# Context attention of a decoder: max units and shifts in one stream over all blocks, 128-row tiles in the first maxima, values made in the first norm's block

## What is computed

```python
x = _layernorm(x + _L0_attn_ref(x, ...))          # a Mamba block
x = _layernorm(x + _L0_xattn_ref(x, ctx, ctx, w_q, w_kv, w_concat))
x = _layernorm(x + _L0_ffn_ref(x, ...))           # experts
x = _layernorm(x + _L1_attn_ref(x, ...))          # self attention
x = _layernorm(x + _L1_xattn_ref(ctx, ctx, x, ...))
x = _layernorm(x + _L1_ffn_ref(x, ...))           # experts
```

```python
c = jnp.concatenate([mem, kv], axis=1)            # both are the context
qh = (q @ w_q).reshape(B, L, 16, 8).transpose(0, 2, 1, 3)
k, v = (c @ w_kv)[..., :8], (c @ w_kv)[..., 8:]
attn_prob = softmax(einsum('bhid,bjd->bhij', qh, k) / sqrt(8), axis=-1)
out = einsum('bhij,bjd->bhid', attn_prob, v)
return out.transpose(0, 2, 1, 3).reshape(B, L, 128) @ w_concat
```

## Time and profile before

| | |
|---|---|
| median of 3 runs | 2247.23 us (2247.16 to 2249.95) |
| the profiled execution | 2255.29 us, its span 2253.6 us |
| PE matmul busy | 2100.2 us, 93% |
| DVE busy | 1590.2 us, 71% |
| ACT busy | 1319.3 us, 59% |
| POOL busy | 120.0 us, 5% |
| mean granted TensorE clock | 0.952 |

### The profile page before, as it was taken

One profiled execution on the slowest core, in us unless ns is written; L12 is line 12 of the kernel. 1 busy time (PEld: TensorE's weight loads), 2 busy tenths in 40 slices (PEclk: granted clock), 3 DMA queues, 4 the chain that ended last, 5 costly groups with the idle time before them and its releaser, 6 DMA issues. The chain is left out here.

```text
span 2253.6 us, 38636 instructions
## 1 busy us (share of the span) xinstructions
PE 2100.2 (93%) x15240; PEld 995.6 (44%) x15240; DVE 1590.2 (71%) x2158; ACT 1319.3 (59%) x2189; POOL 120.0 (5%) x156
## 2 busy tenths in 40 slices
PE   8777999999999999999999999899589997999898
PEld 5223343333333333333333333477533333777755
DVE  4997578898888988889888882223778873444335
ACT  4232157777777777777777778533247773333421
POOL 1560000000000000000000000000200010000000
PEclk7898599999999999999999999899779999999989
DMA  4110000000000000000000000011000000000011
GB/s 135 56 65 0 0 1 1 1 1 1 1 1 1 1 1 1 1 1 1 1 1 1 1 1 1 13 33 35 1 1 1 0 0 0 1 1 0 1 33 33
DMA packets 22978, 24.59 MB, mean 11 GB/s; under 512 B 5728, under 2 KB 20224, under 8 KB 22576
## 3 DMA queue, kind: packets, MB, share of 16 engines
q1 hardware_dynamic: 21648, 20.44, 3.0%
q10 hardware_dynamic: 1184, 2.10, 0.2%
HBM read 21.81 MB, written 0.59 MB: 10 GB/s over the span
## 5 line engine op out<-in xcount | busy, mean ns | idle before, releaser
L959 DVE TENSOR_REDUCE sb_max_partial<-ps_max_ps 128x1 f32<-128x1024 f32 (+1 forms) x896 | 958.1, 1107 | 110.1 <-PE ps_max_ps L802 104.4
L950 ACT ACTIVATE sb_probs<-ps_score_ps 128x512 f32<-128x512 f32 (+1 forms) x1632 | 885.3, 595 | 237.9 <-PE ps_score_ps L922 195.2
L802 PE MATMUL ps_max_ps<-sb_key_stack,sb_q_stack 64*128 64x512 f32 (+1 forms) x1664 | 608.5, 443 | 21.7 <-DVE sb_max_partial L959 9.1
L922 PE MATMUL ps_score_ps<-sb_q_stack,sb_key_stack 64*128 64x512 f32 x1632 | 592.5, 442 | 1.9 <-issue 0.4
L903 PE MATMUL ps_acc_ps<-sb_probs,sb_val_ones 128*32 128x256 f32 x6528 | 521.4, 391 | 0.9 <-ACT sb_probs L950 0.4
L922 PEld LDWEIGHTS ps_score_ps<-sb_q_stack,sb_key_stack 64*128 64x128 f32 x1632 | 241.0, 185 | 281.1 <-ACT sb_probs L950 266.3
L802 PEld LDWEIGHTS ps_max_ps<-sb_key_stack,sb_q_stack 64*128 64x128 f32 x1664 | 256.9, 188 | 159.1 <-DVE sb_max_partial L959 135.3
L903 PEld LDWEIGHTS ps_acc_ps<-sb_probs,sb_val_ones 128*32 128x32 f32 x6528 | 128.4, 108 | 293.0 <-ACT sb_probs L950 218.6
L1654 DVE TENSOR_REDUCE sb_s_max_partial<-ps_s_max_ps 128x1 f32<-128x512 f32 x256 | 170.2, 690 | 42.5 <-PE ps_s_max_ps L1579 35.7
L1644 ACT ACTIVATE sb_s_probs<-ps_s_score_ps 128x1024 f32<-128x1024 f32 x128 | 131.0, 1024 | 49.0 <-PE ps_s_score_ps L1616 46.6
L1871 DVE TENSOR_SCALAR_CACHE_REDUCE sb_x_scores<-ps_x_score_ps 128x1024 f32<-128x1024 f32 (+1 forms) x56 | 62.1, 1111 | 80.7 <-PE ps_x_score_ps L1812 80.7
(11 more groups left out here) (279 smaller groups left out, 1738.7 us busy)
## 6 DMA issues: line engine op xcount, KB each, us to landing
sb_val<-c_rows SPq DMA_DIRECT2D x16, 512.0 KB, 3.7
sb_e_w<-L_ffn_rW SPq DMA_DIRECT2D x30, 128.0 KB, 2.0
sb_e_w<-L_ffn_W_T SPq DMA_DIRECT2D x24, 128.0 KB, 2.1
sb_ctx_T<-ctx_T SPq DMA_DIRECT2D x1, 1664.0 KB, 7.8
sb_ctx_T<-ctx_T ACTq DMA_DIRECT2D x1, 1538.0 KB, 8.7
sb_x_T<-x_T SPq DMA_DIRECT2D x1, 512.0 KB, 4.0
sb_x_tok<-x ACTq DMA_DIRECT2D x1, 512.0 KB, 11.0
sb_e_w<-L_ffn_sW SPq DMA_DIRECT2D x4, 128.0 KB, 3.7
```

What stands on the lines that cost most here:

```text
L802: ins = nc.tensor.matmul(max_ps[:, u % 2, a:a + n], q_stack[rows(blk), blk // 2, h * P:(h + 1) * P], k.key_stack[rows(blk), c0 + a:c0 + a ...
L922: nc.tensor.matmul(score_ps[:, e % 3, :], k.key_stack[rows(blk), c * P:(c + 1) * P], q_stack[rows(blk), blk // 2, j * HALF:(j + 1) * HALF] ...
L950: nc.scalar.activation(probs[0:n, c % 3, j * HALF:(j + 1) * HALF], score_ps[0:n, e % 3, :], ACT.Exp).then_inc(exp_done, 1)
L959: nc.vector.tensor_reduce(partial[:, h, r:r + 1], max_ps[:, u % 2, 0:RANGES[r][1]], AX.X, ALU.max).then_inc(unit_used, 1)
```

## The change

- **Values**: all 51 value tiles are made on PE in norm0's block, ahead of the turns of the normed tiles; ACT copies them behind the two copies of `x_T`. Mamba no longer makes them or waits for them.
- **Queries**: the high part is now subtracted by PE (a matmul with `minus_low`, a diagonal of -1 and 0, that adds to the same bank), and ACT copies the bank a second time. DVE has no part in it. The order of makes, subtractions and units is given by two tables; jobs start with the eleventh unit.
- **First maxima**: POOL copies block 0's queries of each head into `q_first`, whose lower 64 rows are zero, and block 0's units are matmuls of 128 rows.
- **One stream**: units and shifts of all blocks stand in one list `order`, where the shift of block b follows the second unit of block b+1. `chunk_of` spreads the items from block 1 on over all chunks: the shift of block b comes in chunk 46 of block b-1. Places in `max_ps` go by position in the list, the shift takes one of them, and an item waits until the one two before it was used; for a shift that is `q_ready`. In a chunk the first item stands between scores and `weigh`, the others behind `weigh`.
- **Shift copy**: ACT, not DVE, copies the turned shift into `q_stack`, after the exponentials of the chunk behind the one with the shift. `partial` and `part2` have two buffers.

```diff
+            nc.vector.tensor_scalar(k.minus_low[:], k.ident[:], k.half_sel_q[:], None, ALU.mult)
...
-def residual_norm(k, tag, branch, added=False, store=None, turned=None):
+def residual_norm(k, tag, branch, added=False, store=None, turned=None, on_pe=None, on_act=None):
...
+                if on_act is not None:
+                    on_act(act)
...
+                if on_pe is not None:
+                    on_pe(pe)
...
-                keys.values(pe, w_kv, range(0, 12))
...
-                keys.values(pe, w_kv, range(12, NCH))
...
-                pe.wait_ge(keys.v_taken, 1)
...
-                keys.take_values(dve)
...
-        residual_norm(k, "norm0", out_ps, turned=wide(4))
+        residual_norm(k, "norm0", out_ps, turned=wide(4), on_pe=lambda pe: keys.values(pe, w_kv), on_act=keys.take_values)
...
+            FEW = 2
+            LAG = 1
+            order = [(0, u) for u in range(UNITS)] + [(0, None)]
+            for b in range(1, NB):
+                order += [(b, u) for u in range(UNITS)]
+                if b > 1:
+                    order.insert(len(order) - UNITS + FEW, (b - 1, None))
+            order.append((NB - 1, None))
+            place = {x: i for i, x in enumerate(order)}
...
+            FIRST = place[(0, None)] + 1
+            SHIFT_AT = 46
+            lead = place[(1, None)] - FIRST + 1
+            chunk_of = {}
+            for i, x in enumerate(order[FIRST:]):
+                if i < lead:
+                    chunk_of[x] = i * SHIFT_AT // (lead - 1)
+                else:
+                    chunk_of[x] = SHIFT_AT + (i - lead + 1) * NCH // (UNITS + 1)
+            items_at = [[x for x in order[FIRST:] if chunk_of[x] == g] for g in range(NB * NCH)]
...
+            def free_place(pe, item):
+
+                if place[item] < 2:
+                    return
+                blk, u = order[place[item] - 2]
+                if u is None:
+                    pe.wait_ge(q_ready, blk + 1)
+                else:
+                    pe.wait_ge(unit_used, blk * UNITS + u + 1)
...
+                    if blk == 0:
+                        ins = nc.tensor.matmul(dst, q_first[:, h * P:(h + 1) * P], k.key_stack[:, c0 + a:c0 + a + n],
+                                               start=True, stop=True)
...
             def turn_shift(pe, blk):
 
+                free_place(pe, (blk, None))
                 pe.wait_ge(parts_ready, blk + 1)
                 for h in range(HB):
-                    ins = nc.tensor.transpose(shift_ps[0:2, h * P:(h + 1) * P], part2[:, h, :].bitcast(F32), k.ident[:])
+                    ins = nc.tensor.transpose(max_ps[0:2, place[(blk, None)] % 2, h * P:(h + 1) * P],
+                                              part2[:, blk % 2, h, :].bitcast(F32), k.ident[:])
                 ins.then_inc(shift_turned, 1)
...
+            def subtract_high(pe, i):
+
+                pe.wait_ge(q_high, i + 1)
+                nc.tensor.matmul(q_bank(i), k.minus_low[:], q_rows(i), start=False, stop=True,
+                                 skip_group_check=True).then_inc(q_minus, 1)
...
-            FIRST_JOB = 8
+            FIRST_JOB = 10
...
+            EARLY = 3
+            MADE_AT = {0: 3, 2: 4, 4: 5, 6: 6, 8: 7, **{11 + 5 * i: HB + i for i in range(HB)}}
+            MINUS_AT = {0: 2, 1: 3, 3: 4, 5: 5, 7: 6, 9: 7, **{12 + 5 * i: HB + i for i in range(HB)}}
...
-                    if with_max and c <= LAST:
-                        max_unit(pe, blk + 1, u)
-                        u += 1
-                    if c >= 1:
-                        weigh(pe, blk, c - 1)
+                    for item in items[:1]:
+                        issue(pe, item)
+                    if c >= LAG:
+                        weigh(pe, blk, c - LAG)
                     elif blk > 0:
-                        weigh(pe, blk - 1, NCH - 1)
-                    if with_max and c in after_weighing:
-                        max_unit(pe, blk + 1, u)
-                        u += 1
-                    if with_max and c == NCH - 2:
-                        turn_shift(pe, blk + 1)
+                        weigh(pe, blk - 1, NCH - LAG + c)
+                    for item in items[1:]:
+                        issue(pe, item)
...
+            def take_shift(act, blk):
+
+                act.wait_ge(shift_turned, blk + 1)
+                lo = HALF_P * (blk % 2) + TERMS
+                nc.scalar.copy(q_stack[lo:lo + 2, blk // 2, :], max_ps[0:2, place[(blk, None)] % 2, :]).then_inc(q_ready, 1)
...
+                    if blk < NB - 1 and blk * NCH + c == chunk_of[(blk + 1, None)] + 1:
+                        take_shift(act, blk + 1)
...
                 @block.tensor
                 def _(pe):
...
+                    make_queries(pe, 0)
+                    for i in range(EARLY - 1):
+                        make_queries(pe, i + 1)
+                        subtract_high(pe, i)
...
                         if u % NR == 0:
-                            pe.wait_ge(q_done, u // NR + 1)
+                            pe.wait_ge(first_ready, u // NR + 1)
...
+                @block.gpsimd
+                def _(pool):
+                    nc.gpsimd.memset(q_first[HALF_P:P, :].bitcast(F32), 0.0)
+                    for h in range(HB):
+                        pool.wait_ge(q_done, h + 1)
+                        nc.gpsimd.tensor_copy(q_first[0:HALF_P, h * P:(h + 1) * P],
+                                              q_stack[0:HALF_P, 0, h * P:(h + 1) * P].bitcast(F32)).then_inc(first_ready, 1)
```

More of the change, by code:

```diff
@@ L350, in make, with values @@
         nc.tensor.matmul(self.bank(r), k.wk_rep[:], k.ctx_T[:, c0:c0 + n], start=True, stop=True).then_inc(self.k_made, 1)
-    def values(self, pe, w_kv, chunks):
+    def values(self, pe, w_kv):
         nc, k = self.k.nc, self.k
-        for c in chunks:
+        for c in range(NCH):
             n = P if c < NCH - 1 else TAIL
-            if c in (0, self.CUT):
-                pe.wait_ge(self.ctx_loaded[1 if c else 0], 16)
             ins = nc.tensor.matmul(self.v_ps[0:n, c, :], k.ctx_T[:, c * P:c * P + n], w_kv[:, HD:2 * HD], start=True,
                                    stop=True)
-        if NCH - 1 in chunks:
-            ins.then_inc(self.v_ready, 1)
+        ins.then_inc(self.v_ready, 1)
     def high_on_act(self, act, r):
@@ L807, in max_unit @@
-            def max_unit(pe, blk, u):
-                for a in (0, HALF):
-                    max_half(pe, blk, u, a)
+                free_place(pe, (blk, u))
+                for a in range(0, cols, HALF):
+                    n = min(HALF, cols - a)
+                    dst = max_ps[:, place[(blk, u)] % 2, a:a + n]
+                    if blk == 0:
+                        ins = nc.tensor.matmul(dst, q_first[:, h * P:(h + 1) * P], k.key_stack[:, c0 + a:c0 + a + n],
+                                               start=True, stop=True)
+                    else:
+                        ins = nc.tensor.matmul(dst, q_stack[rows(blk), blk // 2, h * P:(h + 1) * P],
+                                               k.key_stack[rows(blk), c0 + a:c0 + a + n], start=True, stop=True)
@@ L816, in turn_shift, with issue @@
                 ins.then_inc(shift_turned, 1)
+            def issue(pe, item):
+                if item[1] is None:
+                    turn_shift(pe, item[0])
+                else:
+                    max_unit(pe, *item)
             def q_bank(i):
-                return (score_ps[0:SPAN2, i % 4, :] if i % 4 < 3 else acc_ps[0:SPAN2, :]) if i < HB else score_ps[0:SPAN2, i % 2, :]
+                if i < HB:
+                    return score_ps[:, i % 4, :] if i % 4 < 3 else acc_ps[:]
+                return score_ps[:, i % 2, :]
@@ L997, in _ @@
                     for blk in range(NB):
-                        attend(pe, blk, blk < NB - 1)
-                    weigh(pe, NB - 1, NCH - 1)
+                        attend(pe, blk)
+                    for v in range(NCH - LAG, NCH):
+                        weigh(pe, NB - 1, v)
                 @block.scalar
```

110 lines of the change are left out of this document (46 added, 64 removed).

## The result

The changed kernel took 2332.06 us (median; 2328.43 to 2334.62) beside 2248.59 for the old one on the same chip: ratio 1.0362, 95% interval 1.0331 to 1.0392, slower by 83.5 us. The forecast was 2351, in a range of 2240 to 2450. The profiled execution has a span of 2328.6, 75.0 above that of the old profile (2253.6).

The account below looks back on a forecast made before the run. PE was taken to bound the attention. Values -3.1, first maxima -34.9, stream +44 and clock +98 sum to +104 us on the median 2247.23: 2351, range 2240 to 2450 (the forecast's own 2295 to 2400).

Parts of the forecast that it names:

- Values beside norm0: Value matmuls moved from Mamba to norm0: Mamba ends 15.0 us earlier, norm0 pays 11.9, together -3.1 (-8.7 to +1.9).
- First maxima: First query to first score, at full clock: 78.4 us against 113.3, -34.9 (-38 to -28; 0 if the clock stays low).
- The stream: Units and shifts spread over all attention blocks: 161 us against 117, +44 (+38 to +50), before the clock's cost.
- (a): Attention chunks with two units: 12 x 0.83 us in block 0, 5 x 0.83 = 4.15 in each other.
- (b): Chunks 44 to 50: six units on the scores' own 64 rows no longer hidden, 0.46 us each, 2.8 a block.
- (c): Chunk 47: second unit behind the shift waits for ACT's copy; PE idles 2.0 us, chunk takes 3.88, +2.65.
- (d): Clock falls at each of 14 stalls at chunk 47, rising some 2.4 ordinary chunks later: 7.0 us a stall, 98 in all.
- Rival C: No stall at chunk 47, as ACT's shift copy is done before PE asks: 2222 us (2205 to 2235); chance 0.12.
- B: Rival: the clock holds through the stalls at chunk 47: 2253 us (2240 to 2266); chance 0.14.
- D: Rival: clock falls and does not rise inside a block: +150 to +585 for the 98, 2400 to 2840; chance 0.14.

Follow-up runs that it names:

- experiment 7: Values back in Mamba, in a kernel with the changed start and old attention blocks: 2218.58 us; values alone moved in the old kernel: 2236.34 us, ratio 0.9956.
- experiment 6: Changed kernel with 64-row tiles in the first maxima: 2342.75 us; then changed start with old attention blocks, but the queries' subtraction back on DVE: 2226.93 us.
- experiment 1: Changed kernel with ACT's copy of the shift taken one chunk earlier, behind the exponentials of chunk 46: 2222.67 us, ratio 0.9895.
- experiment 2: Early units (chunks 44 to 50) on the other 64 rows: changed kernel with ACT's shift copy one chunk earlier, 2196.37 us; changed kernel with stall kept, 2259.68 us.
- experiment 5: Changed kernel's first part (values, queries, first maxima) with the old kernel's attention blocks: 2218.07 us, ratio 0.9867.
- experiment 4: Changed kernel with ACT's shift copy one chunk earlier, plus two extra ACT copies behind chunk 25's exponentials: 2252.07 us, ratio 1.0032.
- experiments 2 and 3: The latter of the two: changed kernel with the weighing of chunk 46 issued ahead of the waiting unit at chunk 47; 2318.84 us, ratio 1.0303.

## Why the prediction was right, and where it was off

**Values beside norm0** (-15.0 + 11.9 = -3.1). Norm0's first statistics come at 171.62 instead of 186.85 (-15.2), the first query at 191.05 instead of 193.47 (-2.4). The 102 records took 17.63 for the forecast 16.5, about 4.3 us of it at full clock (forecast 5):
```profile
170.17 17.63 PE L363 MATMUL ps_mamba_ps<-sb_w_kv,sb_ctx_T 128*128 128x8 f32 x102 [0.33 <-PEq L499]
187.73 1.97 PE L202 MATMUL ps_mamba_ps<-sb_ident,sb_x_tok 128*128 128x128 f32 x8
```
Busy time and clock over the same records:
```profile
170.20:174.50 4.30, 4.30 (x39) 4.30 (x40) 3.89 (x20) 1.42 (x2) 0.00 (x0) 1.00 0.00 0
174.50:187.80 13.30, 13.30 (x66) 13.24 (x66) 2.27 (x9) 0.00 (x0) 0.00 (x0) 0.50 0.01 2
```
(The late group of value matmuls in the old trace has 78 records, where the prediction counts 76; no term uses it.) Right in its parts; as a gain on the whole kernel it shows only in the old first maxima (experiment 7).

**First maxima** (78.4 from first query to first score). Measured 270.36 - 191.05 = 79.3: 5.5 to the first unit (forecast 7.4), 67.9 to the end of the last reduce (65), of which 13.0 are the first ten units (13) and 54.9 the other 46 (52), 5.9 behind it (6.0). The size was right, the reason for the full clock half right. I had it that full-height tiles take away the half-empty work that kept the clock low; experiment 6 shows 64-row tiles at full clock too, once the subtraction is on PE. The height of the tiles alone is worth 8.5 us, not the clock's share of 34.9. The rule weighed there, that a change of tiling mode drains the engine (the Trainium skill, TensorEngine Tiling, Key Properties), asked for a fall from 59 to 49 over the last 46 units. In the runs they took 61.0 with 64-row tiles (experiment 6) and 54.9 with 128-row tiles: the direction agrees, 6 of the 10 us are there, and that a drain is what costs them isn't shown.

**The stream.** (a) and (b): without stall and fall the attention is 5.7 longer than before (experiment 1), where the terms gave 44 - 14 x 2.2 = 13. That comes from (b) in the main: forecast 2.8 a block, measured 2.1 (experiment 2). I had priced all six chunks at 0.46; three of them cost that, chunk 46 cost 0.57, and chunks 48 and 50 only 0.24 and 0.12, while at chunk 47 the same rows gave 0.22 back. (c): chunk 47 takes 3.88, as forecast, in the six blocks where the clock is still full through it, and 4.81 in the other eight, the 0.9 more that (d) had for it; 3.88 against experiment 1's 1.59 is 2.3 for the stall, forecast 2.2. Rival C, which is experiment 1 in all but name, had been priced at 2222 and measured 2222.67. That close a hit is luck: C took 38 off for the first part and put 13 on for the stream, where the runs have 30 by the ratio (experiment 5) and 5.7.

**(d) The clock** was the term mis-sized. It fell at each of 14 stalls, as forecast. The attention grew by 1234.4 - 1129.6 = 104.7 from experiment 1, 7.5 a stall; less 2.3 for the stall itself, 5.2 are left for the clock, 73 in all instead of 98. Chunks 48 and 49 at low clock took 3.01, as priced. Three things were too dear: the clock rose in the second chunk of the next block (the first took 2.17, the second 1.38 to 2.08) and not after 2.4 chunks; in six of the blocks it fell only during chunk 48; and chunk 50, with its 260-column unit, took 2.37 and not 3.0. The other eight look like block 3, where the unit behind the stall already runs at half clock and S(48) comes 4.8 after S(47):
```profile
574.70 0.62 PE L954 MATMUL ps_score_ps<-sb_q_stack,sb_key_stack 64*128 64x512 f32 x2
577.34 1.22 PE L836 MATMUL ps_max_ps<-sb_key_stack,sb_q_stack 64*128 64x512 f32 x2 [2.02 <-ACT sb_q_stack L974]
...
579.50 1.22 PE L954 MATMUL ps_score_ps<-sb_q_stack,sb_key_stack 64*128 64x512 f32 x2
```
The 2.4 chunks were a choice between a quick rise (42 us in all) and none (45 for each stall); no row of the old trace gave them, so that the sum came this near is in part luck.

So -25 of the 32 us by which the attention's growth missed the forecast is this term, and -7.5 is (b) with (a).

**The rivals.** B fell: the clock fell at 41 of 42 stalls of 1.5 to 2.3 us (and at the 14 of experiment 6's first kernel, 2.0 each). The Trainium skill (TensorE: Matmul & The Clock Gate, the table on why this matters) warns only of longer idle gaps; here the measurement decides, and it speaks against reading that as leave for shorter ones. Only experiment 4's 1.1 us pauses behave by it. D fell: the clock was back early in each next block. That S and M then fill both halves of the array fits experiment 2, where the same from chunk 48 on cut the low stretch to 3.4 or 6.8 us, but wasn't tested by itself. D's price left a factor out: 45 chunks at 0.925 more in 13 blocks are 541 us at most, not 585.

**The sum.** In the profiles +75.0 against +104; on the medians +83.5, as the old kernel's profiled execution was 6.7 above its median of 2248.59 and the changed kernel's 1.3 below its own. The terms of the first part come from that profile, which may be why they promise more than the 30 us of the ratio. 2332 lies in the forecast's own range of 2295 to 2400.

## What to carry to other kernels

When a step joins a stream that shares a buffer ring, look up who frees its place and behind what that engine gives it: here one index moved ACT's copy by a chunk and was worth 109 us of 2332. Price a stall of a busy TensorE with the clock that may follow it; here that was 5.2 us on top of 2.3, and how dear it is depended on the work behind it. Work that was free because it ran on other rows of the array is not free once a reordering puts it on the same ones.

## What the runs showed of the hardware

- Pauses of 1.5 to 2.3 us beside the shift came with a fall to 1.2 GHz, 41 in 42 over the changed kernel and experiments 2 and 3, and 14 in 14 in experiment 6; pauses of 1.1 us in mid-block, once in 15.
- The time at the low level depended on the work behind the pause: 10.2 to 13.7 us with scores and units on the same rows, 3.4 or 6.8 us with them side by side.
- The clock fell 4.3 us into the value matmuls of 8 columns, though PE was busy throughout: the 102 records took 17.63 us, 0.17 each, between 0.11 at full and 0.21 at half clock.
- In the first maxima either full-height tiles or the subtraction on TensorE (with its order) was enough to keep 2.4 GHz in the profiled execution; with neither, the old kernel was at 1.2 GHz for 58.0 us and the old kernel with the values moved for 34.1.
